# mLSTM cross-attention and fp4 FFN on one core: tiles of 64 tokens of two batches in place of 128 tokens of one

## The chip, the core and the metric

The kernel runs on one core of a Trainium2 chip. Its engines have an instruction stream each: PE (TensorE, matmul), DVE (VectorE), ACT (ScalarE), POOL (GpSimd) and SP (SyncE, which here issues nearly all the DMAs). They wait for one another through semaphores. The metric is the device time of one launch in microseconds (us). All arithmetic outside the quantised matmuls' f16 operands is float32.

## What is computed

`x` and `ctx_1024` are [8, 1024, 512]: 8 batches of 1024 tokens. The attention part is an mLSTM with 8 heads of 64 (NH, DH): queries from layer-normed `x`, keys and values both from `ctx`. The result is added to `x`, layer-normed and sent through a gated FFN 512 -> 1408 -> 512, whose inputs and weights are rounded blockwise to fp4 values.

```python
def attention(q, k, v):                       # q = layernorm(x), k = v = ctx
    gate_in = concat([q, k, v], -1)
    ig = gate_in @ igate_w.T + igate_b;  fg = gate_in @ fgate_w.T + fgate_b   # per head
    log_f_cum = cumsum(log_sigmoid(fg))
    log_D = where(ltr, log_f_cum[s] - log_f_cum[t] + ig[t], -inf)
    m = max(log_D, -1);  D = exp(log_D - m)
    C = (q @ k.T / 8) * D
    n = maximum(abs(sum(C, -1)), exp(-m))
    h = (C / (n + eps)) @ v                   # then a norm over each head, times norm_w
...
y = x + attention(...)
z = fp4_linear(layernorm(y), w_gate), fp4_linear(layernorm(y), w_up)
out = y + fp4_linear(silu(z[0]) * z[1], w_down)
# fp4_linear rounds both operands in blocks of 16: scale = max|x| / 6, grid 0 .. 6
```

The kernel computes attention chunk by chunk: inside a tile with the decay matrix D, and against everything earlier through a state matrix per head (St, 64 x 65: the 65th column is the normalizer) that is decayed and added to after each tile.

## The kernel before

**Tiles.** A tile is 128 tokens (P) of one batch. Tile t belongs to batch t % 8 (its `slot`) and to the chunk t // 8 of 128 tokens, so 64 tiles (NT) and each batch comes back every 8 tiles; `t.has(8)` marks the waits on the state of 8 tiles ago. Heads are handled in pairs: head 2c + par lies in rows 64 par to 64 par + 63 of the array, c from 0 to 3 (HC).

**Turns.** The program is a software pipeline written out by hand. A turn u runs, on each engine, pieces of several tiles: `t0` is tile u, `t1` tile u - 1, and so on to `t11`. A list of calls per engine (`pe_turn`, `dve_turn`, `act_turn`, `pool_turn`, `sp_turn`) is the order; another list per engine (`pe_start` and so on) holds the beginning, in which the weights are quantised as well. No scheduler moves anything: what stands in a list behind a waiting call waits with it.

**PE's turn**: `gu` of t8 (gate and up products, three column pieces, L523), in the middle of it, in every fourth turn, `gate_mm` and `pick_mm` of t1 (L594: gate rows of four tiles are gathered by matmuls with 0/1 matrices); then `u` of t6: L616 is query times old state, in quarters of the array (64 rows x 64 columns), L622 is D times v, 128 rows by 64 columns; then `st_mm` of t6 (L634, the tile's k v products that go into the state), `down` of t9 in three pieces (L654 to L656) with the transpose `row_T` of the gate rows (L501, every fourth turn) after the first, and last `qk` of t5 (L539, the scores). The scores lie in the PSUM banks R0 and R1 (512 columns each, par 0 and 1), u in R2 and R0, the state sums in R1, `down` in a bank of its own.

**DVE** multiplies scores by D (`dve_C`, L1328, one for each par), multiplies gate and up products (`dve_h`, L1336), updates the state (`dve_St`, L1498: new state = old state times a decay + sum, one instruction for each c), and does the larger part of the quantising (`h_lo`, `x_lo` L1387). **ACT** makes D from the broadcast maxima `mb` (`act_D`, L741), applies silu (L794), copies u out of PSUM (`uc`, L935), makes `hz` (L915) and loads function tables: `preload_act_table_set` (L1005) in each turn. **POOL** masks D (`pool_mask`, L1095), scales v (`vc`, `vk`) and the queries (`xw`).

**SP** loads and stores: `xqT` and `hqT` are DMA transposes of the quantised operands, which PE needs for gu and down; `cn` the context rows; `wb` and `mb` the decay rows and maxima, each a row in DRAM broadcast over partitions; `cf`, `xh`, `xb`, `xzb` feed the transposed q and k; `out_dram<-ob` is the store. All loads of x and ctx come straight from the inputs, one per tile of 128 rows.

## Time and profile before

| | |
|---|---|
| three runs | 1754.49, 1754.5, 1754.88 us; median 1754.5 |
| the profiled execution | 1753.9 us, its span 1752.2 us |
| PE busy | 1679.3 us, 96% |
| DVE busy | 1637.0 us, 93% |
| ACT busy | 1297.4 us, 74% |
| POOL busy | 1154.9 us, 66% |
| DMA | 240.60 MB, mean 137 GB/s |

Busy time is the time in which an engine has at least one instruction under way; the rest is waiting. Shares of the whole span are an average over stages, so the rows further down are of single turns and single steps. A line number L with an operation stands for a source line of the kernel, and `out<-in` names the tensors. "xN" counts the records: a float32 matmul leaves two records, an f16 matmul one. The distance from the start of one group of matmuls to the start of the next is what it keeps PE occupied; the duration beside it includes the time in which the last one drains under the next.

### The profile page before, as it was taken

What the parts mean: (1) busy time and instruction counts of PE and PEld (TensorE: products, weight loads), DVE (VectorE), ACT (ScalarE), POOL (GpSimd) and SP (SyncE); (2) the same over time, 40 slices, a digit from 0 to 9 for tenths busy, and PEclk for the clock granted to TensorE, in tenths of its full rate; (3) what the DMA queues carried; (4) which work ended last, traced back from release to release, by engine and by line L of the source; (5) the groups of instructions that cost most, each with busy time, mean ns of one, the idle gap of its engine ahead of it and who ended that gap; (6) DMA issues with size and microseconds to landing.
All of it is one profiled execution on the core that took longest, in us unless ns stands there. A gap on an engine that the chain in (4) does not pass through costs nothing.

```text
span 1752.2 us, 41405 instructions
## 1 busy us (share of the span) xinstructions
PE 1679.3 (96%) x13633; PEld 898.6 (51%) x13633; DVE 1637.0 (93%) x3455; ACT 1297.4 (74%) x2696; POOL 1154.9 (66%) x1188
## 2 busy tenths in 40 slices
PE   4568999999999999999999999999999999999998
PEld 3434555555555555555555555555555555555544
DVE  8998999999999989999998999999899999999996
ACT  7777777777777777787777778777777877767652
POOL 8876767567666766766666666666666666757663
PEclk9689999999999999999999999999999999999999
DMA  6446656566566656656665675665567566654423
GB/s 213 138 95 140 143 140 150 132 149 151 130 153 139 148 133 147 157 132 147 142 143 134 146 160 130 148 144 142 132 149 157 131 147 144 138 113 101 111 68 71
DMA packets 574454, 240.60 MB, mean 137 GB/s; under 512 B 507520, under 2 KB 514176, under 8 KB 574240
## 3 DMA queue, kind: packets, MB, share of 16 engines
q1 hardware_dynamic: 574240, 237.96, 58.4%
q8 instruction: 108, 1.77, 0.4%
q14 instruction: 106, 0.87, 0.2%
HBM read 140.35 MB, written 31.72 MB: 98 GB/s over the span
## 4 chain that ended last, share of the span: by engine, by line
PE 88%; DMA 0%; DVE 0%; ACT 0%; issue 0%; DVEq 0%
PE bank L523 50%; PE bank L654 9%; PE bank L656 8%; PE bank L655 8%; PE bank L622 4%; PE bank L539 4%; PE bank L616 2%; PE bank L634 2%; PE bank L584 1%; PE bank L594 0%; DMA xqT<-xqs 0%; DMA work<-stage 0%; PE bank L501 0%; DVE stage L1312 0%; DVE stage L1336 0%; DVE ob L1294 0%
## 5 line engine op out<-in xcount | busy, mean ns | idle before, releaser
L523 PE MATMUL bank<-wgTh,xqT 128*128 128x512 f16 (+1 forms) x1536 | 556.3, 362 | 7.5 <-DMA xqT<-xqs 6.4
L523 PE MATMUL bank<-wuTh,xqT 128*128 128x512 f16 (+1 forms) x1536 | 555.3, 362 | 0.0
L1102 POOL TENSOR_TENSOR stage<-stage,hs 128x512 f32<-128x512 f32 (+1 forms) x192 | 214.8, 1119 | 140.2 <-DVE stage L1317 138.5
L523 PE MATMUL bank<-wgTl,xqT 128*128 128x512 f16 (+1 forms) x768 | 277.8, 362 | 0.0
L523 PE MATMUL bank<-wuTl,xqT 128*128 128x512 f16 (+1 forms) x768 | 277.8, 362 | 0.0
L654 PE MATMUL bank<-wdTh,work 128*128 128x512 f16 x704 | 267.7, 380 | 3.3 <-DMA work<-stage 3.3
L655 PE MATMUL bank<-wdTl,work 128*128 128x512 f16 x704 | 267.1, 379 | 0.0
L656 PE MATMUL bank<-wdTh,work 128*128 128x512 f16 x704 | 267.0, 379 | 0.0
L523 PEld LDWEIGHTS bank<-wgTh,xqT 128*128 128x128 f16 x1536 | 150.2, 98 | 169.0 <-issue 10.9
L523 PEld LDWEIGHTS bank<-wuTh,xqT 128*128 128x128 f16 x1536 | 150.5, 98 | 147.4 <-issue 0.5
L1157 POOL TENSOR_TENSOR stage<-stage,hinv 128x512 f32<-128x512 f32 (+1 forms) x192 | 212.6, 1119 | 14.1 <-DVE hinv L1416 7.4
L1091 POOL TENSOR_TENSOR sch<-ve,mhalf 128x8 f32<-128x8 f32 x64 | 105.9, 1655 | 165.0 <-DVE ve L1538 164.8
L794 ACT ACTIVATE stage<-bank,wfix 128x512 f32<-128x512 f32 (+1 forms) x192 | 124.7, 649 | 102.6 <-PE bank L523 101.8
L1371 DVE TENSOR_TENSOR stage<-stage 128x512 f16<-128x512 f32 (+1 forms) x192 | 159.1, 829 | 25.2 <-ACT stage L784 25.2
L1140 POOL TENSOR_TENSOR xn<-xn,xs 128x512 f32<-128x512 f32 x64 | 68.8, 1075 | 138.6 <-DVE xn L1383 136.8
L794 ACT ACT_TABLE_LOAD x123 | 157.8, 1283 | 2.4 <-issue 0.3
L741 ACT ACTIVATE D<-mb,cols 128x128 f32<-128x128 f32 x512 | 156.5, 388 | 1.0 <-DMA mb<-max_dram 0.3
L915 ACT ACTIVATE work<-stage 128x512 bf16<-128x512 f32 (+1 forms) x192 | 112.3, 585 | 50.4 <-POOL stage L1157 48.2
L1336 DVE SCALAR_TENSOR_TENSOR stage<-bank,wfix,stage 128x512 f32<-128x512 f32 (+1 forms) x192 | 134.7, 701 | 12.3 <-ACT stage L794 12.3
L1312 DVE SCALAR_TENSOR_TENSOR stage<-work,stage 128x512 f32<-128x512 bf16 (+1 forms) x192 | 123.3, 666 | 7.5 <-ACT work L915 7.3
L800 ACT ACTIVATE xz<-xn 128x512 bf16<-128x512 f32 x64 | 40.2, 628 | 115.2 <-DVE xn L1375 115.2
L1341 DVE TENSOR_REDUCE ham<-stage 128x32 f32<-128x512 f32 (+1 forms) x192 | 121.0, 631 | 1.7
(210 smaller groups left out, 3656.5 us busy)
## 6 DMA issues: line engine op xcount, KB each, us to landing
mb<-max_dram SPq DMA_DIRECT2D x64, 512.0 KB
x<-in_x_dram SPq DMA_DIRECT2D x64, 256.0 KB, 2.9
wb<-warp_dram SPq DMA_DIRECT2D x128, 128.0 KB, 3.1
cn<-in_ctx_dram SPq DMA_DIRECT2D x64, 256.0 KB, 3.1
out_dram<-ob SPq DMA_DIRECT2D x64, 256.0 KB, 2.4
xb<-in_x_dram SPq DMA_DIRECT2D x60, 256.0 KB, 2.8
xh_dram<-xb SPq DMA_DIRECT2D x55, 256.0 KB, 2.3
xzb<-xh_dram SPq DMA_DIRECT2D x220, 64.0 KB, 2.5
```

The lines of the kernel that those rows point to most:

```text
L523: i = e.matmul(o[:, 0:width], x, w[:, c, n0:n0 + width], start=first and k < 2, stop=last and k >= 4)
L654: e.matmul(acc[:, :], hi, wdT[0][:, c0 + c, :], start=(c0 + c == 0), stop=False)
L655: e.matmul(acc[:, :], hi, wdT[1][:, c0 + c, :], start=False, stop=False)
L656: i = e.matmul(acc[:, :], lo, wdT[0][:, c0 + c, :], start=False, stop=(c0 + c == IC - 1))
L741: i = e.activation(D[:, par, c, :], mb[:, h, :], ACT.Exp, bias=bias[:, h:h + 1], scale=-1.0)
L794: e.activation(sl[:, n0:n0 + w], pair(t, n)[0][:, 0:w], ACT.Silu, scale=wfix[:, 0:1]).then_inc(s_silu[n], 1)
L1102: e.tensor_tensor(blocks(hx[:, n0:n0 + w]), blocks(hx[:, n0:n0 + w]), per_block(hs2[:, n0 // BLOCK:(n0 + w) // BLOCK]), ALU.mult).then_inc ...
L1157: e.tensor_tensor(blocks(hx[:, n0:n0 + w]), blocks(hb[:, n0:n0 + w]), per_block(hinv[:, n0 // BLOCK:(n0 + w) // BLOCK]), ALU.mult).then_in ...
L1312: e.scalar_tensor_tensor(hx[:, n0:n0 + w], hz[:, n0:n0 + w], MAGIC, hx[:, n0:n0 + w], ALU.max, ALU.add).then_inc(s_h_t[n], 1)
L1336: e.scalar_tensor_tensor(hb[:, n0:n0 + w], pair(t, n)[1][:, 0:w], wfix[:, 1:2], sl[:, n0:n0 + w], ALU.mult, ALU.mult).then_inc(s_h[n], 1)
L1341: e.tensor_reduce(ham[:, n0 // BLOCK:(n0 + w) // BLOCK], blocks(hb[:, n0:n0 + w]), AX.X, ALU.max, apply_absolute_value=True).then_inc(S_[" ...
L1371: e.tensor_tensor(hqs[n][:, 1, :], hx[:, n0:n0 + w], hqs[n][:, 0, :], ALU.subtract).then_inc(s_h_lo[n], 1)
```

## The change

**Tiles.** A tile holds 64 tokens (S2) of each of two batches, 2p and 2p + 1 with p = t % 4, from chunk t // 4. A pair of batches comes back every 4 tiles, so the state recurrence, and that of the running maximum `mc`, goes over 4 tiles instead of 8. There are 4 state tensors of two batches each in place of 8.

**PE.** Scores of a tile are 64 x 64 for each head and batch: 16 matmuls of a quarter of the array each in place of 8 of half. The new part of u and the state sums are in quarters too, with the contraction over 64 rows instead of 128; the sums of the second batch go into a second bank (`state_sum`), which is a gate bank of tile t - 2, hence the new wait on s_silu1 in st_mm, and one on St in gu. In u the old part of batch 1 runs ahead of that of batch 0, and a wait on PE's own s_u_old stands before the first new one of batch 1. pick_mm is 8 matmuls instead of 2, row_T is 8 instead of one transpose.

**The others.** D is half as large (`mb_D` holds the maxima and D). The two masks cover the lower 64 partitions or all 128, the first has to be done before the second, and both products with D wait for both. The state update is 8 instructions instead of 4, all on DVE. Gate rows are [64, 64] instead of [32, 128]. The table preload runs only in the turns in which the gates of a quad are computed. wb comes in four loads, mb and cn in two, the store in two.

**Staging.** In every fourth turn ACT issues, first of all, five DMAs that copy x and ctx from DRAM to DRAM, `x_tiles` and `c_tiles`, in the tile's order (4 tiles each; tiles from 12 on for x, from 8 on for ctx); the loads of xb, x1, cn and cf then read these copies. The start lists of all engines are reordered in a few places.

```diff
-    max_dram = nc.dram_tensor("max_dram", [NT, NH * P], F32, kind="Internal").ap()
+    max_dram = nc.dram_tensor("max_dram", [NT // 4, GR * S2], F32, kind="Internal").ap()
+    x_tiles = nc.dram_tensor("x_tiles", [NT, P, E], F32, kind="Internal").ap()
+    c_tiles = nc.dram_tensor("c_tiles", [NT, 3 * S2, E], F32, kind="Internal").ap()
...
-        ST = R1[:, 0:HC * DA].rearrange("p (c d) -> p c d", d=DA)
+        def state_sum(t, b):
+            if b == 0:
+                bk = R1[:, 0:HC * DA]
...
+                bk = pair(t.back(2), 1)[0][:, 0:HC * DA]
...
-                e.transpose(RT, rows[:, :], ident[:, :]).then_inc(S_["row_T"], 1)
+                for k in range(2):
+                    e.matmul(RT[HALF[k], 0:GR].rearrange("s (n r) -> s n r", n=2), rows[:, 0, :],
+                             ident[:, :].rearrange("p (n k r) -> p k n r", n=2, k=2)[:, k], start=True, stop=True)
+                for k in range(2):
+                    e.matmul(RT[HALF[k], 3 * QR:4 * QR], rows[:, 1, :], ident[:, GR + QR * k:GR + QR * (k + 1)], start=True, stop=True)
...
+                if t.has(3) and t.back(-1).live(NT):
+                    e.wait_ge(S_["St"], t.done(-1))
...
             for c in range(HC):
-                for par in range(2):
-                    r = slice(par * DH, (par + 1) * DH)
-                    i = e.matmul((R0, R1)[par][:, c * P:(c + 1) * P], cT[r, t.slot, c, :], xT[r, t.slot, c, :], start=True, stop=True)
+                for b in range(2):
+                    for par in range(2):
+                        r = slice(par * DH, (par + 1) * DH)
+                        i = e.matmul((R0, R1)[par][HALF[par ^ b], c * S2:(c + 1) * S2], cT[r, t.slot, c, HALF[b]], xT[r, t.slot, c, HALF[b]],
+                                     start=True, stop=True)
...
-                for k in range(2):
-                    i = e.matmul(gates(t)[1], pick[:, k, :], gpart[:, k, :], start=(k == 0), stop=(k == 1))
+                for out_rows, at in ((gates(t)[1], slice(0, 2 * GR)), (gates(t)[2], slice(2 * GR, 3 * GR))):
+                    for k in range(2):
+                        for b in range(2):
+                            i = e.matmul(out_rows, pick[:, k, b, at], gpart[:, k, HALF[b]], start=(k + b == 0), stop=(k + b == 2))
...
+            def old(c, b):
+                for par in range(2):
+                    r = HALF[par]
+                    i = e.matmul(U[par][HALF[b], c, :], xw[r, b, c, :], St[t.p][r, b, c, :], start=(c == 0), stop=False)
+                return i
+
+            def new(c, b):
+                for k in range(2):
+                    r, par = HALF[k], k ^ b
+                    i = e.matmul(U[par][HALF[b], c, :], D[r, par, c, :], vc[t.parity][r, 2 * c + par, :], start=False, stop=(c == HC - 1))
+                return i
...
-                    i = e.matmul(R1[par * DH:(par + 1) * DH, c * DA:(c + 1) * DA],
-                                 cn[:, h * DH:(h + 1) * DH], vk[:, h, :], start=True, stop=True)
+                    for b in range(2):
+                        h, r = 2 * c + par, HALF[par ^ b]
+                        i = e.matmul(state_sum(t, b)[HALF[par], c, :], cn[r, h * DH:(h + 1) * DH], vk[r, h, :], start=True, stop=True)
...
+        def act_stage_c(e, g):
+            if g > 2:
+                e.wait_ge(S_["c_tiles"], 48 * (g - 2))
+            at = slice(g * S2, (g + 1) * S2)
+            src = ctx_in[:, at, :].rearrange("(p b) s e -> b p s e", b=2)
+            for k in range(3):
+                e.dma_start(c_tiles[4 * g:4 * g + 4, k * S2:(k + 1) * S2, :], src[k % 2]).then_inc(S_["c_tiles"], 16)
+
+        def act_stage_x(e, g):
...
+                e.dma_start(x_tiles[4 * g:4 * g + 4, k * S2:(k + 1) * S2, :], src[k]).then_inc(S_["x_tiles"], 16)
+
         def act_turn(e, u):
             tn = Tile(u + 1)
+            g = (u + 3) // 4
+            if u % 4 == 1 and 4 * g < NT:
+                act_stage_x(e, g)
+                act_stage_c(e, g)
...
-            e.preload_act_table_set(EXP_LN)
+            if t1.live(NT) and t1.slot % 4 == 3:
+                e.preload_act_table_set(EXP_LN)
...
-            e.tensor_tensor(D[:, par, :, :].rearrange("p c s -> p (c s)"), (R0, R1)[par][:, :],
+            e.tensor_tensor(D[:, par, :, :].rearrange("p c s -> p (c s)"), (R0, R1)[par][:, 0:HC * S2],
...
-            for c in range(HC):
-                i = e.scalar_tensor_tensor(St[t.slot][:, c, :], St[t.slot][:, c, :], wb[:, c, P - 1:P], ST[:, c, :], ALU.mult, ALU.add)
+            for b in range(2):
+                for c in range(HC):
+                    i = e.scalar_tensor_tensor(St[t.p][:, b, c, :], St[t.p][:, b, c, :], wb[:, b, c, S2 - 1:S2], state_sum(t, b)[:, c, :], ALU.mult, ALU.add)
```

On PE, u and the state sums of one tile stand so in before's order (the names in brackets are semaphores that the instruction waits for; xN counts the matmuls that follow alike):

```order
L616 MATMUL bank<-St,xw 64x65 [waits s_C0,s_xw,s_St]
L616 MATMUL bank<-St,xw 64x65 x15
L622 MATMUL bank<-vc,D 64x65 [waits s_C1,s_vc]
L622 MATMUL bank<-vc,D 64x65 x15
L634 MATMUL bank<-vk,cn 64x65 [waits s_vk,s_cn_in]
L634 MATMUL bank<-vk,cn 64x65 x7
L654 MATMUL bank<-wdTh,work 128x512 [waits s_out,s_hqT0]
```

and so in the order of the change:

```order
L689 MATMUL bank<-St,xw 64x65 [waits s_C0,s_xw,s_St]
L689 MATMUL bank<-St,xw 64x65 x13
L689 MATMUL bank<-St,xw 64x65 [waits s_C1,s_vc]
L689 MATMUL bank<-St,xw 64x65
L695 MATMUL bank<-vc,mb_D 64x65 x4
L695 MATMUL bank<-vc,mb_D 64x65 [waits s_u_old]
L695 MATMUL bank<-vc,mb_D 64x65 x11
L729 MATMUL bank<-vk,cn 64x65 [waits s_silu1,s_vk,s_cn_in]
L729 MATMUL bank<-vk,cn 64x65 x15
L748 MATMUL bank<-wdTh,work 128x512 [waits s_out,s_hqT0]
```

The wait for the second product with D moved two matmuls ahead, a wait on PE's own work came in between, and the state sums, 16 matmuls for 8, wait for a silu as well.

ACT at the start of a turn with the staging copies, before:

```order
L741 ACTIVATE D<-mb,cols 128x128 x8
L866 ACTIVATE xb<-xb,nb,rs 128x512
L915 ACTIVATE work<-stage 128x512
L927 ACTIVATE mw<-mw,mc 32x128
L756 ACTIVATE nm<-sum 128x1
```

and in the change:

```order
L833 ACTIVATE mb_D<-mb_D,cols 128x64 x8
L1081 DMA x_tiles<-in_x_dram 4x2x16384 x2
L1074 DMA c_tiles<-in_ctx_dram 4x2x16384 x3
L958 ACTIVATE xb<-xb,nb,rs 128x512
L1007 ACTIVATE work<-stage 128x512
L1018 ACTIVATE mw<-mw,mc 64x64
L848 ACTIVATE nm<-sum 128x1
```

Five DMA issues stand ahead of xh (L958) and hz (L1007); the shape of one copy, 4x2x16384, is eight contiguous pieces of 16384 float32.

SP's queue, one turn of before:

```order
L384 DMA_TRANSPOSE xqT<-xqs 128x8x128
L410 DMA cn<-in_ctx_dram 128x512
L402 DMA wb<-warp_dram 64x512 x2
L364 DMA cf<-in_ctx_dram 32x16x32 x4
L345 DMA xh_dram<-xb 128x512
L339 DMA xb<-in_x_dram 128x512
L353 DMA xzb<-xh_dram 32x16x32 x4
L310 DMA out_dram<-ob 128x512
L319 DMA x<-in_x_dram 128x512
L328 DMA_TRANSPOSE work<-stage 128x8x128 x2
L372 DMA mb<-max_dram 128x1024
L328 DMA_TRANSPOSE work<-stage 128x6x128
```

and of the change:

```order
L430 DMA_TRANSPOSE xqT<-xqs 128x8x128
L459 DMA cn<-c_tiles 128x4x64 x2
L449 DMA wb<-warp_dram 64x256 x4
L408 DMA cf<-c_tiles 32x16x32 x4
L387 DMA xh_dram<-xb 128x512
L378 DMA xb<-x_tiles 128x512
L395 DMA xzb<-xh_dram 32x16x32 x4
L341 DMA out_dram<-ob 64x512 x2
L352 DMA x<-x_tiles 128x512
L364 DMA_TRANSPOSE work<-stage 128x8x128 x2
L418 DMA mb_D<-max_dram 64x512 x2
L364 DMA_TRANSPOSE work<-stage 128x6x128
```

The sequence is the same; there are five issues more, and four kinds of load read the staged copies.

## Rows read from the trace of the kernel before

**Rows 1.** The page's first part: busy us, share of the span, instructions.

```profile
PE 1679.3 (96%) x13633; PEld 898.6 (51%) x13633; DVE 1637.0 (93%) x3455; ACT 1297.4 (74%) x2696; POOL 1154.9 (66%) x1188
```

**Rows 2.** The chain that ended last, share of the span by engine.

```profile
PE 88%; DMA 0%; DVE 0%; ACT 0%; issue 0%; DVEq 0%
```

**Rows 3.** Windows of four PE turns: us, busy of PE, PEld, DVE, ACT, POOL, clock, DMA share, GB/s.

```profile
858.54:883.40 24.86, 24.86 (x204) 13.13 (x203) 24.55 (x52) 19.85 (x43) 17.59 (x19) 1.00 0.70 158
883.40:908.26 24.86, 24.86 (x204) 13.13 (x203) 23.97 (x51) 18.81 (x40) 16.83 (x18) 1.00 0.65 149
908.26:933.12 24.86, 24.86 (x204) 13.12 (x203) 23.86 (x51) 18.82 (x40) 16.71 (x18) 1.00 0.64 146
933.12:960.50 27.38, 27.38 (x241) 14.61 (x240) 23.86 (x57) 20.29 (x46) 15.75 (x17) 1.00 0.53 122
```

**Rows 4.** Timeline of PE: start us, duration us, line, operation, stationary and moving shapes, records.

```profile
806.25 1.16 PE L539 MATMUL bank<-xT,cT 64*128 64x128 f32 x16
807.34 0.39 PE L523 MATMUL bank<-wgTh,xqT 128*128 128x512 f16 x1
...
821.71 0.70 PE L616 MATMUL bank<-St,xw 64*64 64x65 f32 x32
822.33 1.15 PE L622 MATMUL bank<-vc,D 128*64 128x65 f32 x32
823.32 0.64 PE L634 MATMUL bank<-vk,cn 128*64 128x65 f32 x16
823.89 0.39 PE L654 MATMUL bank<-wdTh,work 128*128 128x512 f16 x1
...
845.52 0.60 PE L594 MATMUL bank<-gpart,pick 128*96 128x128 f32 x4
845.96 0.33 PE L523 MATMUL bank<-wgTh,xqT 128*128 128x384 f16 x1
...
853.76 0.27 PE L501 MATMUL bank<-ident,rows 128*128 128x128 f32 x1
853.87 0.38 PE L654 MATMUL bank<-wdTh,work 128*128 128x512 f16 x1
```

**Rows 5.** Groups by form, DVE: total busy us, mean ns of one, idle before.

```profile
L1336 DVE SCALAR_TENSOR_TENSOR stage<-bank,wfix,stage 128x512 f32<-128x512 f32 x128 | 95.3, 744 | 12.0 <-ACT stage L794 12.0
L1336 DVE SCALAR_TENSOR_TENSOR stage<-bank,wfix,stage 128x384 f32<-128x384 f32 x64 | 39.4, 616 | 0.3 <-ACT stage L794 0.3
L1328 DVE TENSOR_TENSOR D<-bank,D 128x512 f32<-128x512 f32 x128 | 86.5, 675 | 1.8 <-POOL D L1095 1.8
L1498 DVE SCALAR_TENSOR_TENSOR St<-St,wb,bank 128x65 f32<-128x65 f32 x256 | 55.0, 277 | 0.9 <-issue 0.6 <-PE bank L634 0.3
```

**Rows 6.** The same view, ACT's table preload.

```profile
L1005 ACT ACT_TABLE_LOAD x61 | 78.3, 1283 | 1.1
```

**Rows 7.** Timeline around xqT and nr; the third is the page's DMA landing.

```profile
801.54 0.68 DVE L1387 TENSOR_TENSOR xqs<-xn,xqs 128x512 f16<-128x512 f32 x1
...
802.25 1.24 SPq L384 DMA_TRANSPOSE xqT<-xqs  x1
...
xqT<-xqs SPq DMA_TRANSPOSE x64, 3.1
...
824.22 0.17 DVE L1508 SCALAR_TENSOR_TENSOR nr<-uc,cols 128x8 f32<-128x8 f32 x1 [0.60 <-ACT uc L935]
```

**Rows 8.** Timeline: SP's issue of cn, silu 1, and hz with DVE's next step.

```profile
803.58 0.53 SPq L410 DMA_DIRECT2D cn<-in_ctx_dram  x1
...
849.53 0.69 ACT L794 ACTIVATE stage<-bank,wfix 128x512 f32<-128x512 f32 x1
...
859.25 0.63 ACT L915 ACTIVATE work<-stage 128x512 bf16<-128x512 f32 x1 [0.20 <-POOL stage L1157]
...
861.25 1.28 DVE L1312 SCALAR_TENSOR_TENSOR stage<-work,stage 128x512 f32<-128x512 bf16 x2
```

**Rows 9.** The page's DMA part: queue and kind, packets, MB, share of 16 engines.

```profile
q8 instruction: 108, 1.77, 0.4%
```

300 lines of the change are left out of this document (182 added, 118 removed).

## The prediction

> **What bounds the kernel now.** I read four views, in this order. The shares of busy time name two candidates: PE is busy for 96% of the span and DVE for 93% [rows 1]. The chain of work that ended last settles it: 88% of it is PE, the rest spread thin [rows 2]. The windows of four successive turns show how: PE is busy in every nanosecond at full clock, turns of 24.86, 24.86, 24.86 and 27.38 us, 101.96 us together, while DVE has 24.55, 23.97, 23.86 and 23.86 us of work in them [rows 3]. So DVE idles 0.3 to 1.0 us in three turns and 3.5 in the fourth, the one with the gates. What a step costs PE I take from the timeline as the distance from its start to the start of what follows, since matmuls overlap [rows 4]. The 64 tiles make 16 such cycles, of which I count 14 with all their steps; start and end cut the other two. One microsecond off PE in each turn is therefore worth 64 us, as long as everything that PE waits for also comes earlier. The other engines' distances to PE are the question, so I read them last [rows 6, 7, 8].
>
> **PE, each turn.** The scores take 806.25 to 807.34 = 1.09 us for 16 records of 64 rows by 128 columns [rows 4]. After: 32 records in array quarters. The old-state part of u is such a case, 32 records on quarters in 821.71 to 822.33 = 0.62 us [rows 4]. I take 0.62: **-0.47 us**. The two others that change form are the new part of u, 0.99, and the state sums, 0.57 [rows 4]. With the old part they cost 2.18. After, all three are 32 records of the quarter form, 3 x 0.62 = 1.86 if the halves overlap as in the old part. The staggered order leaves half of the array idle at both ends of u, and its new wait on PE's own work (s_u_old) drains part of the pipe; 2 of 16 steps at 0.04 each is 0.08. So 1.94: **-0.24 us**, between -0.1 (a full drain of 0.14 more) and -0.35. Together -0.71 a turn (-0.6 to -0.85).
>
> **PE, each fourth turn.** pick goes from two matmuls, 4 records in 0.44 us [rows 4], to eight, 16 records, with 64 moving columns instead of 128. At the old 0.11 each they cost 1.76 (+1.3), at half of it 0.88 (+0.4). I take +0.8, since the moving side has half the columns but the stationary side stays as tall. row_T goes from one transpose in 0.11 us (853.76 to 853.87 [rows 4]) to eight matmuls, 16 records, none over 64 columns wide; at the quarter form's 0.02 to 0.04 each that is 0.3 to 0.7, so +0.45 (0 to 0.6). Together +1.25 (+0.4 to +1.9, mostly 0.9 to 1.7).
>
> PE's sum for four turns is -2.84 + 1.25 = -1.6 us: 14 x -1.6 = **-22 us** (-13 to -30).
>
> **DVE.** A width of 512 in place of 384 costs 744 - 616 = 128 ns in one of its operations [rows 5], 0.13 us per 128 elements. The two products with D go from 512 to 256: -0.27 each, -0.54. The state update doubles from four instructions to eight; each is 277 ns busy [rows 5], but four take 0.86 us, so one more costs about 0.2 from start to start: +0.86. Each turn gets **+0.3 us**; the gate operations, 64 columns for 128, give some 0.35 back in the fourth, an estimate: five of them at half of the 0.13. DVE then needs 24.85, 24.3, 24.2 and 23.8 us, where PE's turns are 24.15 (24.86 - 0.71) three times and 27.9 once. DVE falls behind by 0.7 + 0.1 = 0.8 us and catches up in the gate turn. Whether PE feels that depends on the margins. The transpose of xqT is issued when x_lo ends at 802.22 and takes 3.1 us to land, 805.4, against its use at 807.34 [rows 4, 7]: 2.0 us. qk, 0.47 shorter, now lies in this stretch, which leaves 1.5. The 0.8 fits in. What follows u on DVE (nr) does not come late by itself: it waits 0.60 us for ACT, which waits for PE [rows 7], and moves with PE.
>
> **ACT.** The decay's exponentials have half the columns, which I cost at nothing, since nothing waits for them. The table preload of 1.28 us, once a turn now [rows 6], and the reload that it forces stay only in each fourth turn: 2.57 us less in three turns. ACT has 19.9 of 24.86 us of work [rows 3], so nothing of it is on the path, but ACT's answers to PE come a little sooner. At the start of each fourth turn it issues the five staging copies. SP's issue of a 256 KB load took 0.53 us [rows 8], five make 2.6 us, and they stand ahead of xh, of hz 1 and hz 0, for which DVE's next step waits [rows 8]. The work queued there now runs at 859.25; I take it that about 1.0 us of delay reaches DVE (0 if ACT is early, 2.6 if all of it counts), on top of the 0.8 above: 1.8 against a margin of 1.5. Other margins are as thin in that turn (silu 1 ends at 850.22 and st_mm, which waits for it after, starts at 850.59 [rows 4, 8], 0.37 us). I put the give-back at 0.7 us a cycle, 12 cycles with copies: **+8 us** (0 to +15).
>
> **SP's queue.** Its loads of rows split in two where they were one, five issues more a turn (wb two, mb, cn and stored one each), at some 0.55 [rows 8]. cn, wb, cf, xh and xb stand behind one another, so xb's load comes 3 x 0.6 = 1.8 us later; SP idles longer than that ahead of it, and hqT 0 and 1 wait for DVE's h_lo, behind all of these. I cost it at nothing; if SP is late at hqT 0, PE's down waits by up to 1 us a turn, which is part of the second rival. mb moves half the bytes: -256 KB a turn.
>
> **Start and end.** The start lists get three more groups of copies, and fewer and shorter steps: -1 us (-5 to +5).
>
> **Sum.** The profiled run took 1753.9 us (span 1752.2 and 1.7 around it), 0.6 below the median of 1754.5; it fits. 1753.9 - 22.3 + 8 - 1 = **1738.6, say 1739**, own range 1724 to 1750.
>
> **Rival A, the staging copies hold up the transposes: 1830 us.** Each group is 40 pieces of 64 KB from DRAM to DRAM, 2.5 MB. The only packets of comparable size in the trace are those of the instruction queue: 108 of 1.77 MB, 16.4 KB each, and 0.4% of 16 x 1752 us is 112 us, so 1.04 us each [rows 9]. A piece of 64 KB would take 4.2 us. For it: forty of them fill 16 DMA engines for 10.4 us, and fewer engines for longer; the transposes of xqT and hqT, which land in 3.1 us [rows 7], are needed within 5; whatever queues behind even one piece is 4 us late. Against it: DMA is at 0.70 to 0.53 of its capacity [rows 3], which leaves 38 us of all engines idle in a cycle for 10.4, and the loads wait for nothing if the engines serve them between the pieces. If loads wait for the whole group, 10.4 us less the margins of 2 to 3 is 5 to 10 us of idle PE: 12 x 5 = +60 to 12 x 10 = +120, here 1739 + 90 = 1829, say 1830 (1799 to 1859, more if few engines carry the copies). It decides once a transposing load's landing goes from 3.1 to above 5 us.
>
> The Trainium skill ("DMA: Bandwidth & Descriptors", section "Why a DMA increments its semaphore by 16 and not by 1") says that a transfer uses as many engines as the largest number up to 16 that divides its slowest dimension. The copies' slowest dimension is 4; by that rule four engines would carry ten pieces each, an estimate of 42 us, and this rival would reach 1900. The same page's section "Queues, rings and completion order" says that an engine takes turns between queues packet by packet, which would soften it; no row of before shows a copy of this shape.
>
> **Rival B, DVE and the queues take all back: 1752 us (1748 to 1762).** DVE is then 0.3 us a turn dearer and has no room left: 97.1 us of work in a PE cycle of 100.3. If its work has gaps that it can't close in the gate turn, because C, h and St wait there for PE in any case, each cycle gives back 1.2 us instead of 0.7, and SP's lateness at hqT adds 0.1 to 0.2 in each turn, 0.6 a cycle: 14 x 0.5 + 14 x 0.6 = 15 less what is counted twice, 1739 + 13 = 1752. For it: DVE idles only 0.3 us in the first turn [rows 3]. Against it: 3.5 us idle in the gate turn.
>
> **Rival C, quarters don't overlap where both row halves write one bank: 1785 us.** In the new part of u and in the state sums of after, both row halves of the array fill the same bank, in different partitions. In before each row half has a bank of its own in the quarter form, so no row shows the case. If only two of four quarters then run at a time, 32 records cost what 32 with two in flight cost now: 0.99 for the new part, 2 x 0.57 = 1.14 for the sums [rows 4]. Against 0.62 each that is 0.37 + 0.52 = +0.89 a turn, 64 x 0.89 = 57; PE's turns are then no shorter than today, DVE keeps up, and the 8 us of give-back fall away: 1739 + 57 - 8 = 1788, some 1785 with the stagger's 0.08 not counted twice.
>
> The Trainium skill ("TensorEngine Tiling (Array Packing)", section "Restrictions and Gotchas", Gotcha 1) says that different row tiles can't use one PSUM bank at the same time. By that rule rival C would be the outcome; no row of before tells.
>
> **How the numbers follow.** "Same" is within 0.2%, 3.5 us around 1754.5, about what a measurement of this kernel can tell from no change. The forecast has 0.53: 0.50 faster and 0.03 in its tail above 1751. A has 0.25, all slower; the windows of [rows 3] leave room for the copies, but nothing in before shows their form. B has 0.12: 0.02 faster, 0.05 same, 0.05 slower. C has 0.05, slower. A time below 1724 (pick and row_T at their low ends, no give-back) has 0.03, and something slower that I don't see 0.02. Faster 0.50 + 0.02 + 0.03 = 0.55; same 0.03 + 0.05 = 0.08; slower 0.25 + 0.05 + 0.05 + 0.02 = 0.37. The range runs from 1724, the forecast's low end, to 1850: it takes in B, C and most of A, and leaves out 0.03 below and some 0.1 of A above.
>
> **What would show it.** Right: windows of four PE turns with PE still busy throughout, 24.15 three times and near 28; qk's line 0.62 from start to start; u and the state sums 1.94; three of four preloads gone; DVE's idle in the first three turns near zero. A: PE idle behind xqT or hqT in the turn of the copies, their landings above 5 us, DMA share near 1 for 10 us or long packets on a few engines, turns of over 30 us there and forecast turns elsewhere. B: gaps of PE before gu 0, u or down, released by DVE, in turns without copies too. C: u and the sums at 2.5 us or more together. I am wrong outright if PE's turns are no shorter though PE is gapless, or if PE's clock falls in gaps of the copy turn, as it does nowhere in before [rows 3].

## The result, and the profile after

The changed kernel takes **2185.6 us** (median; 2180.0 to 2189.5) beside 1754.5 for the kernel before on the same chip: a ratio of **1.246 (1.243 to 1.249)**, 431 us slower. The forecast was 1739, the range 1724 to 1850. The profiled run took 2180.0, its span 2178.2.

The page of the changed kernel: first part (busy us, share of the span, instructions), the chain that ended last by engine, and queues (packets, MB, share of 16 engines' span).

```profile
PE 1733.5 (80%) x16113; PEld 906.8 (42%) x16113; DVE 1781.6 (82%) x3711; ACT 1153.3 (53%) x2602; POOL 1158.4 (53%) x1196
issue 58%; POOL 32%; DVE 3%; SPq 2%; PE 2%; DMA 2%; ACT 1%; POOLq 1%; DVEq 0%; ACTq 0%
...
q10 hardware_dynamic: 816, 35.65, 3.9%
```

PE held 88% of the chain before [rows 2] and has 2% now. "Issue" is time in which the engine waited for nothing that the profile shows; it holds 58%, so much of the chain has no releaser that the profile names, and the windows have to tell more. Here are two turns of the changed kernel (columns as in [rows 3]), one without and one with the staging copies:

```profile
1404.77:1431.55 26.78, 25.59 (x240) 12.94 (x239) 26.47 (x55) 16.13 (x37) 16.77 (x17) 1.00 0.65 127
...
1462.47:1507.35 44.88, 37.06 (x336) 19.37 (x334) 30.95 (x67) 21.09 (x49) 17.93 (x18) 0.96 0.44 119
```

Against the 24.86 us of [rows 3] there are two different losses. The turn with the copies takes 44.9 us, with PE and DVE both idle for long and the DMA share low. But a turn *without* copies also takes 26.8, and there DVE is busy for 26.47 of 26.78 us: DVE has become the bound, by 2.6 us a turn more than its 23.9.

I cut every span at two starts of scores, that of the ninth tile and that of the last. In the tables "start" is what lies ahead of the first, "mid" between the two, "end" the rest (profiled run, us; start and end to within 0.7). The ratio is against the kernel before on the same chip; its interval is worth 2 to 7 us on either side.

| kernel | median | ratio (95%) | start | mid | end |
|---|---|---|---|---|---|
| before | 1754.5 | | 271.6 | 1400.2 | 80.4 |
| after | 2185.6 | 1.246 (1.243 to 1.249) | 363.0 | 1729.3 | 85.9 |

### The profile page after: what moved, and what is told of

Same layout as the page of the kernel before. It is cut to its first block, busy times and chain, and to the rows that moved or that the text cites. A ratio compares the mean times of both kernels' runs of the same rounds, so it can differ in the third digit from the quotient of the medians.

```text
span 2178.2 us, 47128 instructions
## 1 busy us (share of the span) xinstructions
PE 1733.5 (80%) x16113; PEld 906.8 (42%) x16113; DVE 1781.6 (82%) x3711; ACT 1153.3 (53%) x2602; POOL 1158.4 (53%) x1196
## 3 DMA queue, kind: packets, MB, share of 16 engines
q10 hardware_dynamic: 816, 35.65, 3.9%
## 4 chain that ended last, share of the span: by engine, by line
issue 58%; POOL 32%; DVE 3%; SPq 2%; PE 2%; DMA 2%; ACT 1%; POOLq 1%; DVEq 0%; ACTq 0%
POOL stage L1273 6%; POOL stage L1218 4%; POOL mb_D L1211 4%; POOL xw L1251 3%; POOL un L1284 3%; POOL xn L1256 3%; POOL vk L1243 3%; POOL vc L1235 2%; POOL rs L1262 1%; SPq L478 1%; PE bank L592 1%; SPq L465 1%; DMA cf<-in_ctx_dram 1%; POOL nb L1266 0%; DMA xqT<-xqs 0%
## 5 line engine op out<-in xcount | busy, mean ns | idle before, releaser
L592 PE MATMUL bank<-wgTh,xqT 128*128 128x512 f16 (+1 forms) x1536 | 572.3, 373 | 131.4 <-DMA xqT<-xqs 74.7
L592 PE MATMUL bank<-wuTh,xqT 128*128 128x512 f16 (+1 forms) x1536 | 570.2, 371 | 0.0
L592 PE MATMUL bank<-wgTl,xqT 128*128 128x512 f16 (+1 forms) x768 | 285.5, 372 | 0.0
L592 PE MATMUL bank<-wuTl,xqT 128*128 128x512 f16 (+1 forms) x768 | 285.3, 371 | 0.0
L1436 DVE SCALAR_TENSOR_TENSOR stage<-work,stage 128x512 f32<-128x512 bf16 (+1 forms) x192 | 252.9, 1344 | 2.3
L689 PE MATMUL bank<-St,xw 64*64 64x65 f32 x2048 | 54.5, 248 | 186.8 <-DVE mb_D L1447 174.0
L934 ACT ACTIVATE junk<-xb 128x512 bf16<-128x512 f32 x60 | 37.8, 629 | 304.5 <-DMA xb<-x_tiles 293.7
L1235 POOL TENSOR_TENSOR vc<-cn,cols 128x512 f32<-128x512 f32 x64 | 66.8, 1043 | 223.4 <-DMA cn<-c_tiles 194.9
L1741 DVE STREAM_TRANSPOSE cT<-cf 128x512 f32<-128x512 f32 x55 | 38.4, 698 | 175.3 <-DMA cf<-c_tiles 175.3
L1431 DVE SCALAR_TENSOR_TENSOR stage<-work,stage 128x512 f32<-128x512 bf16 (+1 forms) x192 | 118.6, 644 | 40.2 <-ACT work L1007 40.0
L1007 ACT ACTIVATE work<-stage 128x512 bf16<-128x512 f32 (+1 forms) x192 | 112.1, 584 | 69.1 <-POOL stage L1273 68.8
L1490 DVE TENSOR_TENSOR stage<-stage 128x512 f16<-128x512 f32 (+1 forms) x192 | 120.4, 627 | 31.1 <-ACT stage L876 31.1
```

The lines of the kernel that those rows point to most:

```text
L592: i = e.matmul(o[:, 0:width], x, w[:, c, n0:n0 + width], start=first and k < 2, stop=last and k >= 4)
L1007: e.activation(hz[:, n0:n0 + w], hx[:, n0:n0 + w], ACT.Abs, scale=FP4_ONE).then_inc(s_hz[n], 1)
L1431: e.scalar_tensor_tensor(hx[:, n0:n0 + w], hz[:, n0:n0 + w], MAGIC, hx[:, n0:n0 + w], ALU.max, ALU.add).then_inc(s_h_t[n], 1)
L1436: e.scalar_tensor_tensor(hx[:, n0:n0 + w], hz[:, n0:n0 + w], MAGIC, hx[:, n0:n0 + w], ALU.max, ALU.subtract).then_inc(s_h_q[n], 1)
L1490: e.tensor_tensor(hqs[n][:, 1, :], hx[:, n0:n0 + w], hqs[n][:, 0, :], ALU.subtract).then_inc(s_h_lo[n], 1)
```

## The experiments

### The staging copies

**The changed kernel without its copies (e1).** The loads of rows read x and ctx directly. In e1 and in every run built on it (e5, e7, e9, e10, e12) they fetch rows of other tokens, so these runs price the steps but don't compute the result.

```diff
-    act_stage_x(e, g); act_stage_c(e, g)      # here and in the start list
-    e.dma_start(xb[:, :], x_tiles[t.first])
+    e.dma_start(xb[:, :], x_flat[at_flat(t, 0, P), :])   # x1, c alike
```

> The change without the staging copies: xb, x1, cn and cf are loaded with the same shapes and the same number of DMAs straight from x and ctx, from the places of before's tiles (so the data belong to other tokens, and the output is not the reference's), and ACT issues no DMA. Theory A, the copies are the whole loss: PE-bound turns come back and the time is my forecast without the give-back, 1725 to 1745. Theory A + P, the copies are one part and the other is that DVE is held up by POOL in three of four turns (the second h_q takes 3.97 us instead of 0.69 there): the cycle of four turns is then 3 x 26.8 + 30.9 = 111.3 us against 101.96 before, and the time 1754 + 14 x 9.3 = 1885 (1860 to 1900). Rival, the copies cost nothing and loads wait for something else: 2180.

1937.6 us, 1.105 (1.103 to 1.107); start 312.1, mid 1533.9, end 84.8. So the copies are worth 248 us (195 mid, 51 start), and **183 us are left that have nothing to do with them**. That lies outside all three ranges expected; the nearest, which has both copies and a stall of DVE, had 131 us left.

**The kernel before with the same copies (e4),** into DRAM that nobody reads.

```diff
 def act_turn(e, u):
+    g = (u + 3) // 4
+    if u % 4 == 1 and 4 * g < NT:
+        act_copies(e, g)      # the five DMAs of one group
```

> The kernel before with the change's copies added and nothing else: twelve groups of five DMAs, 4x2x16384, issued by ACT at the start of each fourth turn, into DRAM that nobody reads. If the copies alone stop the loads on the engines that they share, each group costs what the change's copy turn is longer than its neighbours, 44.9 - 26.8 = 18 us, and up to 20 since before has no idle time: 1754 + 12 x 18 to 20 = 1970 to 1995. If the loss comes only from loads that wait for the copied tiles, or from SP's extra loads, it is 1755 to 1770.

2077.8, 1.185 (1.182 to 1.187); start 299.5, mid 1699.5, end 79.9. That is above the 1970 to 1995 expected. Only the turn with the copies changes, from 24.86 to some 52 us: 12 x 27 = 324. Two rows of this kernel's trace, the first gate-up matmul of a turn with copies and the waits view (total us, times, longest), and the source view's landing times of the transposing load:

```profile
1044.69 0.61 PE L526 MATMUL bank<-wgTh,xqT 128*128 128x512 f16 x1 [24.67 <-DMA xqT<-xqs]
PE bank L526 <- DMA xqT<-xqs: 304.3, 16, 34.4
DMA to landing us min/median/max: 3.0/3.1/38.5
```

The median of [rows 7] still stands, but the longest is 38.5 us: the condition of rival A. In the changed kernel the same load's longest is 13.8, and more of the loss lies in what SP issues. Its queue in the turn with the copies (start us, duration us, line, operation):

```profile
1481.61 1.23 SPq L430 DMA_TRANSPOSE xqT<-xqs  x1
1482.94 1.50 SPq L459 DMA_DIRECT2D cn<-c_tiles  x2
1484.55 22.85 SPq L449 DMA_DIRECT2D wb<-warp_dram  x4
```

And ACT's queue beside the first of these, one of its five copies:

```profile
1482.11 0.62 ACTq L1081 DMA_DIRECT2D x_tiles<-in_x_dram  x1
```

ACT gets rid of its DMAs in 0.6 us each, as forecast. SP, half a microsecond later, needs 22.85 us to issue four loads that take about half a microsecond apiece elsewhere [rows 8]. What SP has behind them, cf and xb, is issued some 20 us late. cn, issued before them, lands late: its longest landing is 28.7 us, its median 2.8 (source view of L459). The waits of the changed kernel name their users:

```profile
ACT junk L934 <- DMA xb<-x_tiles: 293.7, 51, 23.9
POOL vc L1235 <- DMA cn<-c_tiles: 194.9, 11, 19.1
DVE cT L1741 <- DMA cf<-c_tiles: 175.3, 12, 18.2
PE bank L689 <- DVE mb_D L1447: 174.0, 13, 20.3
```

cn and cf: 11 and 12 waits of up to 19 and 18 us, about one for each group. PE stands behind DVE, DVE behind cf.

**The copies on 16 engines (e2), and in smaller pieces on four (e3).**

```diff
 # e2: q=16 (16 x 4 x 2048 elements); e3: q=4 (4 x 4 x 8192)
-e.dma_start(x_tiles[...], src[k])
+e.dma_start(x_tiles[...].rearrange("p (q s) e -> q p (s e)", q=16),
+            src[k].rearrange("p (q s) e -> q p (s e)", q=16))
```

> The change with the same bytes copied in the same five DMAs from the same place, only that each is laid out as 16x4x2048 instead of 4x2x16384: sixteen groups of four pieces of 8 KB in place of eight pieces of 64 KB. If what stands still is the four DMA engines that carry the large pieces (40 pieces of 2.42 us on four engines, 25 us), the copies spread over sixteen and take about 6 us, SP's queue doesn't stand, and the time is that of the run without copies within 1.5%: 1885 to 1910. If the copied bytes themselves or ACT's five issues are the cost, it stays above 2050.

> The change with each copy laid out as 4x4x8192: the same bytes, pieces of 32 KB instead of 64 KB, and the slowest dimension still 4. If the number of engines is what matters, forty becomes eighty pieces of half the time on the same four engines, the 25 us stay and so does the time: 2160 to 2190. If the size of a piece is what blocks a load behind it, the loads wait half as long each and the time falls half of the way to the 16x4x2048 form: 2060 to 2100.

e2: 1964.9, 1.120 (1.116 to 1.123); start 321.0, mid 1555.9, end 86.2; the median is above the 1885 to 1910 expected. e3, as expected if the engines count: 2179.8, 1.241 (1.237 to 1.246), that is unchanged; 366.5, 1729.2, 85.7. The copies' queue in e2, then in e3:

```profile
q10 hardware_dynamic: 5440, 35.66, 5.3%
```

```profile
q10 hardware_dynamic: 1360, 35.65, 3.9%
```

The changed kernel moves 35.65 MB in 816 packets. 35.65 MB are 544 pieces of 64 KB; the other 272 are 68 copies x 4. In e2 there are 5440 = 68 x (64 + 16), in e3 1360 = 68 x (16 + 4). The part that doesn't grow with the pieces reads as one packet for each engine that a copy uses: 4, 16, 4. The time agrees: 3.9% of 16 x 2178.2 us is 1359 us over 544 pieces, **2.5 us a piece**; a group is 40 pieces, on four engines 25 us; in e2 5.3% of 16 x 1963.1 us, over 13.6 groups and 16 engines, is 7.7 us. So e3 is as slow as the kernel it was made from, though its pieces are smaller, and e2 gets 221 of 248 us back. The number of engines decides; halving the pieces on the same four does nothing. e2's pieces are also smaller, 8 KB, and that size on four engines was not run. The Trainium skill ("DMA: Bandwidth & Descriptors", section "Why a DMA increments its semaphore by 16 and not by 1") gives the rule, the largest number up to 16 that divides the slowest dimension of both sides; here, with a slowest dimension of 4, 16 and 4, the trace agrees in all three.

The records of single packets show how the loads are held up. In the changed kernel a window out of a group of copies (columns as in [rows 3]) has a DMA share of 0.25, four engines of 16:

```profile
1488.00:1504.00 16.00, 13.42 (x57) 5.99 (x58) 7.39 (x15) 4.32 (x8) 3.56 (x4) 0.89 0.25 103
```

All through it three or four pieces of 64 KB are under way, 2.42 us each, and ahead of each of the 28 that start from 1489.7 to 1504.9 us one packet of 256 B of SP's queue is served. So the four engines do take turns between the two queues, but one small packet waits for one large piece. From 1495.0 to 1504.3 SP's queue moves 18 packets of 256 B and nothing else. The new loads of cn consist of such packets, 512 each (128 x 4 runs of 64 float32). Over 16 engines that is 32 per engine, an estimate, where ten pieces on each of the four and five semaphore writes leave room for some 15. In e3 there are 20 pieces and as many writes on each, still fewer than 32, and the longest landing of cn is 28.1 us; in e2 it is 11.9. The Trainium skill (same page, section "Queues, rings and completion order") lets an engine take turns between its queues packet by packet, and this trace agrees. Why SP's *issuing* stands as well, up to 12 us for one load, is open.

### What is left without copies: 183 us

In e1 DVE is again the engine that is full (94% of the span). One place stands out in every kernel with the changed code. In the changed kernel, DVE's stretch around the scores at 884.45, and POOL's beside it:

```profile
884.15 1.28 DVE L1431 SCALAR_TENSOR_TENSOR stage<-work,stage 128x512 f32<-128x512 bf16 x2
885.47 4.58 DVE L1436 SCALAR_TENSOR_TENSOR stage<-work,stage 128x512 f32<-128x512 bf16 x2
```

```profile
885.33 0.55 POOL L1226 TENSOR_TENSOR rs<-ss,mhalf 128x1 f32<-128x1 f32 x1 [1.73 <-ACT ss L869]
885.84 0.83 POOL L1211 TENSOR_SCALAR_AFFINE_SELECT mb_D<-mb_D 64x512 f32<-64x512 f32 x1
886.65 1.05 POOL L1218 TENSOR_TENSOR stage<-stage,hs 128x512 f32<-128x512 f32 x1
887.66 0.83 POOL L1273 TENSOR_TENSOR stage<-stage,hinv 128x384 f32<-128x384 f32 x1
888.46 1.04 POOL L1235 TENSOR_TENSOR vc<-cn,cols 128x512 f32<-128x512 f32 x1
```

The two halves of h_q at L1436 take 4.58 us together, 1.3 for the pair at L1431. The second of them alone lasts 3.97 us, not 0.69: it ends at 890.05, 0.55 us after POOL's run of back-to-back instructions (888.46 + 1.04). DVE instructions of over 2 us after the first 250 us: none in the kernel before, 47 in the changed one, 58 in e1, 249 us together in e1. Each of these 105 ends 0.04 to 0.55 us after the end of a run of POOL.

Four things could do this: the order of the work on POOL, the eight state updates, the missing table preloads (ACT answers earlier), and the masks, of which the second now covers 64 partitions. One run each.

**POOL's order (e5).** e1 with the h_qs that waits for DVE put first.

```diff
 # pool_turn: as before for the masks and rs2, then
+    pool_h_qs(e, t9, 1)
     pool_h_qs(e, t9, 0)
     pool_hx(e, t9, 2)
     pool_vc(e, t6)
-    pool_h_qs(e, t9, 1)
     pool_xw(e, t6)
```

> The run without copies (data of other tokens, as there) with one edit in POOL's turn: h_qs 1 is called ahead of h_qs 0, so that POOL waits for DVE's second h_q instead of running mask, h_qs 0, hx 2 and vc without a gap while DVE stands. If POOL's unbroken run is what holds DVE up for 3.3 us, the second h_q takes under 1.5 us, DVE has room again and the time falls by up to 14 x 3 x 2.7 = 113 to 139 us, at most down to PE's own pace: 1735 to 1780. If DVE is simply out of room because of the eight state updates, the order changes nothing or costs: 1870 to 1900.

1853.6, 1.057 (1.055 to 1.059); 309.5, 1458.1, 84.7. 84 us less, between the two ranges expected. Long instructions fall from 58 to 18: the 40 or so on h_q are gone, and what is left is on xs (4.99 us each), which was long 17 times in e1 as well. Where POOL's run starts and what DVE has there matters; why it shuts DVE out is not told by this.

**The state updates: e1 with four of eight (e7), the kernel before with four more (e6).**

```diff
 # e7, dve_St
-for b in range(2):
+for b in range(1):
 # e6, dve_St of the kernel before
+for c in range(HC):
+    e.scalar_tensor_tensor(Sx[:, c, :], St[t.slot][:, c, :], wb[:, c, P - 1:P], ST[:, c, :], ALU.mult, ALU.add)
```

> The run without copies (data of other tokens), with the state update of the second batch left out, so that DVE issues four updates as before instead of eight and the second batch's state stays zero. If the doubled update is what makes DVE late and sets off the stall, the second h_q falls back to 0.7 us and the time to PE's pace and the longer start: 1754 - 22 + 40 = 1772, 1760 to 1800. If the stall comes from ACT and POOL being earlier in their turn (half the decay matrix, no preload), it stays and only 0.8 us a turn is saved: 1938 - 50 = 1885.

> The kernel before with four more state-update instructions on DVE in each turn, into a tile that nobody reads: DVE's added load of the change, alone. By the sum of my prediction DVE then needs 25.4, 24.8, 24.7 and 24.7 us in turns of 24.86 three times and 27.4 once, it gives back in the gate turn, and the time is 1754 to 1765. If DVE, once late against POOL by half a microsecond, is shut out for the length of POOL's unbroken run, turns go to 26 to 27 us in three of four: 1754 + 14 x 5 to 8 = 1825 to 1866, and the line of the second h_q shows durations near 3 to 4 us.

e7: 1911.4, 1.090 (1.087 to 1.092); 311.9, 1515.2, 82.9; 57 long instructions, nearly all on xs now. e6: 1773.7, 1.012 (1.010 to 1.014); 274.1, 1416.9, 81.9; none. Four updates cost 19 to 26 us, 0.3 to 0.4 a turn, and cause no stall. e7 saves half of what was expected even without the stall going, e6 costs more than the 0 to 11 expected.

**The table preloads: e1 with one each turn (e9), the kernel before with one each fourth (e8).**

```diff
 # e8; e9 is the reverse
+if t1.live(NT) and t1.slot % 4 == 3:
     e.preload_act_table_set(EXP_LN)
```

> The run without copies (data of other tokens) with the preload back in each turn. If the missing preload is what lets POOL overtake DVE, the second h_q falls back to 0.7 us and the time to 1790 to 1850, with the longer start. If the order of events is set elsewhere (half the decay matrix, the masks, DVE's longer update), it stays at 1930 to 1945.

> The kernel before with the table preload only in the turns with gates, as in the change, and nothing else. If ACT, 2.6 us less busy in three turns, brings POOL's run of six instructions ahead of DVE's second h_q, before gets the same stall and the time rises by 1 to 2 us in each of these turns: 1790 to 1850. If the preload has no part in it (its 1.28 us lie in ACT's idle time): 1750 to 1756.

e9: 1923.2, 1.097 (1.095 to 1.098); 310.7, 1525.9, 84.6; 57 long ones. e8: 1754.0, 1.000 (0.999 to 1.001); 271.1, 1400.2, 81.7. Not this either: 14 us in the one, where at least 88 were expected of a cause, nothing in the other. Leaving out three of four table loads brings the kernel before nothing.

**The mask over 128 partitions (e10), and the kernel before with a mask over 64 (e11).** A small edit each; both leave values of D masked wrongly.

```diff
 # e10, on e1
-part = mb_D[0:S2 * (k + 1), 1, :, :]
+part = mb_D[:, 1, :, :]
 # e11, on the kernel before
+n = P if par else P // 2
-e.affine_select(out=D[:, par, :, :], in_=D[:, par, :, :], ...
+e.affine_select(out=D[0:n, par, :, :], in_=D[0:n, par, :, :], ...
```

> The run without copies (data of other tokens) with the second mask of each tile over 128 partitions instead of 64 (so that rows 64 to 127 of the decay matrix are masked wrongly); the order of all calls is unchanged. All 58 stalls of DVE above 2 us in the run without copies began in a POOL run with this mask in it, and kernels with masks over 128 partitions alone had none. If an instruction over 64 partitions is what keeps DVE out of the gaps in POOL's run, the stalls above 2 us vanish and the time falls by 2 to 3 us a turn: 1938 - 56 x 2.5 = 1800 (1790 to 1850). If it is the timing alone, the stalls stay and so does the time, 1925 to 1945.

> The kernel before with its second mask (par 0) over 64 partitions instead of 128, so that the rest of that half is left unmasked; nothing else. If the 64-partition form is what keeps DVE out, xs, which waits 0.7 us in before, waits for the whole of POOL's run, 4 to 5 us, in every turn: DVE then needs 28 us a turn, 1754 + 56 x 3 = 1920 (1850 to 1960). If the form has no part in it: 1750 to 1757.

e10: **1794.6**, 1.024 (1.022 to 1.026); 307.7, 1403.0, 82.0; no long instruction. e11: **1908.0**, 1.088 (1.086 to 1.090); 287.1, 1537.4, 81.8; 57 of them. Both are as expected if the form is the cause. Widening this one mask to 128 partitions takes 143 us off e1, narrowing it to 64 adds 154 us to the kernel before, and the long instructions go and come with it. In e10 the same place reads, on DVE and on POOL:

```profile
1052.55 1.75 DVE L1436 SCALAR_TENSOR_TENSOR stage<-work,stage 128x512 f32<-128x512 bf16 x2
```

```profile
1052.91 0.84 POOL L1211 TENSOR_SCALAR_AFFINE_SELECT mb_D<-mb_D 128x512 f32<-128x512 f32 x1
1053.73 1.48 POOL L1218 TENSOR_TENSOR stage<-stage,hs 128x512 f32<-128x512 f32 x1
```

The instructions meet in the same way; but now DVE gets in after the mask, the pair takes 1.75 us, and POOL's next instruction lasts 1.48 instead of 1.05. The mask itself is no slower over 128 partitions than over 64 (0.84, 0.83). In e11 the victim is xs, which the source view gives as min/median/max ns; the kernel before, then e11, and POOL's run in e11 beside one such xs:

```profile
L1357 DVE TENSOR_SCALAR xs<-xam,rs x64: 227/924/928, 102.0 to 1701.6; 128x32 f32<-128x32 f32 x64
```

```profile
L1358 DVE TENSOR_SCALAR xs<-xam,rs x64: 229/4973/5486, 105.5 to 1856.2; 128x32 f32<-128x32 f32 x64
```

```profile
994.75 4.97 DVE L1358 TENSOR_SCALAR xs<-xam,rs 128x32 f32<-128x32 f32 x1
...
993.89 0.72 POOL L1096 TENSOR_SCALAR_AFFINE_SELECT D<-D 64x512 f32<-64x512 f32 x1
```

The Trainium skill ("SBUF — State Buffer", section "SBUF: two separate sides") says that GpSimd and DVE (in an operation with two SBUF inputs, or in a two-port mode) hold a shared port for a whole instruction, and that the other fully blocks. e10's rows agree: the pair ends at 1054.30, 0.55 us after the mask. The 3.97 and 4.97 us do not: there DVE waits for the end of a run of several instructions. In both runs the mask is the second, right behind a short rs of 128x1. Why an instruction over 64 partitions there does that is open.

### What is left without copies and stall

**e1 with both causes out of the way (e12):** the masks back to back ahead of rs2, where DVE doesn't meet them, e5's order, and in PE's start list the state sums of the third tile ahead of its gate-up.

```diff
 # pool_turn
     pool_mask(e, t6, 1)
+    pool_mask(e, t6, 0)
     pool_rs2(e, t7)
-    pool_mask(e, t6, 0)
 # PE's start list
-pe_gu(e, T[1], 0); pe_st_mm(e, T[2])
+pe_st_mm(e, T[2]); pe_gu(e, T[1], 0)
```

> The run without copies (data of other tokens) with three edits: the two masks one behind the other, h_qs 1 ahead of h_qs 0, and the state sums of tile 2 ahead of gu 0 of tile 1 in the start. It shows what PE's saving is worth when neither copies nor long stalls are there. If the saving of my sum is real, three turns are 24.05 to 24.5 us and the cycle is 100.5 to 101.5 against 101.97, with 38 us of start on top: 1775 to 1795. If DVE is what sets the pace even so, the cycle is above 102.5 and the time 1800 to 1815.

1790.7, 1.021 (1.019 to 1.023); 308.0, 1398.8, 83.2; no long instruction. **The mid part is as long as before (1400.2), and nearly all that is left, 36 us, lies in the start.** Four turns in e12:

```profile
1021.20:1045.40 24.20, 24.17 (x245) 12.47 (x235) 23.89 (x54) 15.88 (x36) 16.03 (x18) 1.00 0.73 135
1045.40:1070.50 25.10, 24.38 (x242) 12.51 (x233) 24.79 (x55) 16.30 (x37) 16.92 (x18) 1.00 0.62 136
1070.50:1099.10 28.60, 28.34 (x309) 15.43 (x298) 27.20 (x64) 20.76 (x47) 18.27 (x19) 1.00 0.59 127
1099.10:1123.10 24.00, 24.00 (x243) 12.40 (x233) 23.73 (x53) 16.18 (x39) 15.67 (x17) 1.00 0.67 136
```

101.90 us, where [rows 3] have 101.96. PE is busy for 100.89; the best turns are as forecast, 24.0 to 24.2, but DVE has 99.6 us of work, not the forecast's 97.1. The groups of DVE in this window of e12 (busy us, mean ns), and behind them those of the kernel before in the same window:

```profile
L1613 DVE SCALAR_TENSOR_TENSOR St<-St,wb,bank 128x65 f32<-128x65 f32 x32 | 6.5, 275 | 0.0
L1496 DVE SCALAR_TENSOR_TENSOR xn<-xz,xn 128x512 f32<-128x512 bf16 x4 | 5.7, 1421 | 0.0
L1526 DVE TENSOR_SCALAR hs<-ham 128x88 f32<-128x88 f32 x5 | 5.3, 1054 | 0.0
L1445 DVE TENSOR_TENSOR mb_D<-bank,mb_D 128x256 f32<-128x256 f32 x8 | 3.3, 411 | 0.0
```

```profile
L1328 DVE TENSOR_TENSOR D<-bank,D 128x512 f32<-128x512 f32 x8 | 5.4, 675 | 0.0
L1379 DVE SCALAR_TENSOR_TENSOR xn<-xz,xn 128x512 f32<-128x512 bf16 x4 | 4.1, 1036 | 0.8 <-ACT xz L800 0.8
...
L1498 DVE SCALAR_TENSOR_TENSOR St<-St,wb,bank 128x65 f32<-128x65 f32 x16 | 3.4, 278 | 0.0
L1409 DVE TENSOR_SCALAR hs<-ham 128x88 f32<-128x88 f32 x4 | 0.8, 193 | 0.0
```

Its own work moved as costed: updates +3.1, the products with D -2.1. But hs takes 1054 ns instead of 193 with the same shape, xn 1421 instead of 1036. These are operations that meet POOL elsewhere in the turn than they used to: 4 x 0.86 + 4 x 0.39 = 5.0 us, of which some is given back in others (xs has its 924 no more). One hs of e12 and POOL beside it:

```profile
1045.61 1.06 DVE L1526 TENSOR_SCALAR hs<-ham 128x88 f32<-128x88 f32 x1
1045.23 2.39 POOL L1273 TENSOR_TENSOR stage<-stage,hinv 128x512 f32<-128x512 f32 x2 [0.42 <-DVE hinv L1533]
```

After the first 300 us, 57 of the 59 hs of e12 start while POOL is in its product with hinv, take 1.0 us or more and end 0.06 to 0.07 us after that instruction (the row above holds two of them). In the kernel before only 7 meet it so, and take 1.0 us too; 48 start during the short nb ahead of it and take 0.2.

**The start: the kernel before with the doubled loads of its first tiles (e13).**

```diff
 # x, x1 (first 12 tiles) and cf in two DMAs, cn (first 8) in four
+for b in range(2):
+    e.dma_start(xb[HALF[b], :], half_rows(x_rows, t, b))
```

> The kernel before with the change's number of loads in the start: x and x1 of tiles below 12 and cf of the first in two DMAs each, cn of tiles below 8 in four; the same bytes, all issued by SP. If SP's queue, which issues without a pause from 110 to 170 us, is what makes the change's start 38 to 40 us longer, this gives 20 to 40 us: 1775 to 1795. If it is the order of the start lists or DVE's waits, 1754 to 1765.

1769.4, 1.010 (1.007 to 1.012); 282.3, 1400.2, 81.8, between the two ranges expected. The start gets 10.7 us longer by the split loads alone (the whole span 12, the median 15): more issues, and cn in runs of 256 B. Mid is untouched. SP is busy issuing for 48 of the 60 us from 110 to 170 in the kernel before. Its transposing load of the second tile's xqT leaves at 133.84 us there, in e13 at 140.97:

```profile
133.84 2.62 SPq L384 DMA_TRANSPOSE xqT<-xqs  x1
```

```profile
140.97 1.24 SPq L398 DMA_TRANSPOSE xqT<-xqs  x1
```

Some 25 us of the start stay unexplained. They are there early: the scores of the fourth tile start at 135.5 us in the kernel before, at 140.7 in e13, at 157.9 in e12.

### Versions that compute everything

**v2:** e2's copies spread over four turns (two of x, then one of ctx in each of three), with e5's order. **v3:** v2 with e12's masks and start. **v4:** v3 with DVE's xs behind xi. **v6:** v3 with one mask for both halves, a product with a stored triangle of zeros and ones over 128 partitions. **v7:** v6 with the state's decay on ACT (eight activations with a scale), and two additions instead of eight updates on DVE.

```diff
 # v6, pool_mask
-e.affine_select(out=part, in_=part, ...)          # twice
+keep = tri[:, :].unsqueeze(1).broadcast_to([P, NH, S2])
+e.tensor_tensor(whole, whole, keep, ALU.mult)     # once
 # v7, act_decay and dve_St
+i = e.activation(St[t.p][:, b, c, :], St[t.p][:, b, c, :], ACT.Identity, scale=wb[:, b, c, S2 - 1:S2])
+i = e.tensor_tensor(St[t.p][:, b, :, :], St[t.p][:, b, :, :], state_sum(t, b), ALU.add)
```

> A complete version: the change with copies of the form 16x4x2048, two in the first turn of four and one in each of the others instead of all five in one, and POOL's turn with h_qs 1 ahead of h_qs 0. If the copies' remaining cost is their density and ACT's five issues in one turn, it comes near the run without copies in the same POOL order, 1854: 1855 to 1880. If each copy costs wherever it stands, it is that plus what separates the 16-engine form from no copies (27 us): 1880 to 1900.

> The complete version with 16-engine copies spread over the turns and POOL's h_qs 1 first (1872 us), with two more edits: POOL runs the two masks one behind the other ahead of rs2, and in PE's start list the state sums of tile 2 stand ahead of gu 0 of tile 1. If the mask between rs2 and h_qs is what still holds DVE's second h_q up for 1.05 us, three turns of four get shorter by up to 1 us, 14 x 3 = -42 at most; DVE waits 9.8 us for those state sums in the start, -5 to -10. So 1820 to 1855. If DVE meets POOL's run elsewhere instead, 1862 to 1875.

> The version before this one with DVE's xs moved behind xi, six instructions later. In the turn behind the gates xs takes 4.99 us instead of 0.55, under POOL's run from mask to xw; of the six instructions that now come first none was held up there for more than 0.6 us. If they run under POOL's run, that turn gains 2 to 3 us: 14 x 2.5 = -35 against the run before. If the hold-up only moves to h_lo, which reads two SBUF operands too, nothing is gained.

> A complete version: 16-engine copies spread over the turns, POOL's h_qs 1 first, the start edit, and in place of the two masks one multiplication of the decay matrix by a stored 0/1 triangle over 128 partitions. POOL saves 0.9 us a turn and runs no instruction over 64 partitions. By the run without copies in the good order (1791) plus what spread copies cost (1872 - 1854 = 18): 1800 to 1815. If DVE's products and POOL's new two-operand instruction hold each other up, 1820 or more.

> The version before this one with the state update shared: ACT multiplies the two states by their decay (eight short instructions behind sq, 1.6 us of its idle time) and DVE adds the sums in two instructions of 260 elements, 0.8 us instead of 1.6. If DVE's load is what keeps the turns above 24.05, the cycle falls from some 102.5 towards PE's 100.4: 14 x 2 = 28 us, 1775 to 1790. If the margins of copies, ACT and POOL set it, nothing or a loss: 1800 to 1820. Neither is expected to beat before, since the start alone costs 37 us.

| kernel | median | ratio (95%) | start | mid | end |
|---|---|---|---|---|---|
| v2 | 1871.7 | 1.068 (1.066 to 1.070) | 313.7 | 1470.7 | 84.9 |
| v3 | 1822.5 | 1.040 (1.038 to 1.042) | 316.0 | 1420.4 | 81.7 |
| v4 | 1823.5 | 1.040 (1.038 to 1.041) | 314.2 | 1422.2 | 83.7 |
| v6 | 1825.8 | 1.042 (1.039 to 1.044) | 315.3 | 1427.2 | 84.0 |
| v7 | 1883.0 | 1.076 (1.072 to 1.080) | 318.0 | 1481.7 | 82.4 |

Spreading seems to bring the copies' price from 27 us (e2 against e1) to 18 (v2 against e5). But in the better order, v3 against e12, the same spread copies cost 32 (8 start, 22 mid), so spreading is not shown to help. v3 is the best complete one, 363 us faster than the change as it was made and still 4% slower than the kernel before: 44 us in the start, 20 mid. v4 gains nothing. v6 has no mask over 64 partitions and is no better than v3, which has no long instruction either. v7 takes work from DVE, but lands far above both of its ranges: DVE now waits for ACT's silu, 79.3 us in all, where in v6 it waits 17.4:

```profile
DVE stage L1481 <- ACT stage L887: 79.3, 68, 2.5
```

## Why the prediction was wrong, step by step

The 431 us come in three parts: copies 248 (changed kernel less e1), the 64-partition mask 143 (e1 less e10), and 40 that e10 has over the kernel before, 36 of them in the start. They add up because each is taken from the kernel that the one before it left; in another order the parts differ (in the kernel before the copies cost 324, the mask 154).

**PE, each turn: right.** The changed kernel's PE, from start to start (columns as in [rows 4]):

```profile
884.45 0.69 PE L609 MATMUL bank<-xT,cT 64*64 64x64 f32 x32
885.08 0.39 PE L592 MATMUL bank<-wgTh,xqT 128*128 128x512 f16 x1
...
899.44 0.74 PE L689 MATMUL bank<-St,xw 64*64 64x65 f32 x32
...
901.27 0.39 PE L748 MATMUL bank<-wdTh,work 128*128 128x512 f16 x1
```

The scores take 0.63 us (forecast 0.62), u and the sums 1.83 (forecast 1.94, within its bounds of 1.83 to 2.08). The best turns are 24.0 to 24.2 (forecast 24.15).

**PE, each fourth turn: right.** In e12:

```profile
1084.23 1.61 PE L670 MATMUL bank<-gpart,pick 128*128 128x64 f32 x16
1085.77 0.34 PE L595 MATMUL bank<-wgTh,xqT 128*128 128x384 f16 x1
...
1093.32 0.34 PE L560 MATMUL bank<-ident,rows 128*64 128x64 f32 x4
1093.90 0.39 PE L751 MATMUL bank<-wdTh,work 128*128 128x512 f16 x1
```

pick 1.54 (+1.10, forecast +0.8, in its bounds), row_T 0.58 (+0.47, forecast +0.45). With 28.25 for such a turn a cycle of PE alone is 100.4, where the working gave 100.36. That it fits so closely is luck: the three turns came out some 0.3 us shorter together, the fourth 0.35 longer.

**DVE: the mechanism was right, the size was not, and the step "the 0.8 fits in" failed.** The +0.3 a turn of its own work held. What I left out is that the durations of [rows 5 to 7] hold beside the POOL work of *their* place. A change that shifts DVE against POOL re-prices operations that it doesn't touch: hs and xn, 5 us a cycle, net 2.5 more than forecast. DVE then needs 99.6 us in a PE cycle of 100.4, with no room for a wait, and the 22 us that PE saves are gone (mid 1398.8 against 1400.2). Rival B named this end for the steady state, DVE without room, but took 13 of the 22 us back and for other reasons; it had 0.12.

**What no step had: 143 us by the mask over 64 partitions.** The change names the mask, and the prediction has no term for POOL at all; its rows say that POOL is idle 7 us a turn. The mask itself takes 0.83 us over 64 partitions as over 128. The step that failed is that the sum gave every DVE instruction a price that doesn't depend on what POOL does beside it.

**ACT's share of the copies: priced at the wrong end.** The issue took 0.6 us each, as costed, and the forecast's +8 us was made of that. The cost lies in the transfer, and in SP, which I had "at nothing": four loads take 21 to 24 us to issue in each of 12 turns.

**Rival A: right in its mechanism, with too low a price.** Rival A named the copies, the loads behind them and the landing of over 5 us (13.8 in the changed kernel, 38.5 in e4). I chose against it on "the loads wait for nothing if the engines serve them between the pieces". The engines do serve them between the pieces, and that is the step that failed: one packet goes between two pieces, so a load of many packets is held for as long as the copies last. The price went wrong in two terms that half cancel: 2.5 us a piece, not 4.2, but on 4 engines, not 16, so 25 us a group, not 10.4. Less the margins of 2 to 3 that is 22; the mid part lost 195 us, 18 for each of the 11 groups in it, where the rival had 5 to 10, and the start, with three groups (one without x), lost 51 more. The sentence with the skill's rule had four engines and 42 us a group, 1900 in all; its engines were right, and with the trace's 2.5 us a piece in place of my 4.2 it comes to the measured 25.

**Rival C: false.** Both row halves write one bank, and the three sets of 32 records, one with separate banks and two without, take 1.83 us together, not the 2.5 or more of the rival. The Trainium skill ("TensorEngine Tiling (Array Packing)", "Restrictions and Gotchas", Gotcha 1), by which different row tiles can't use one PSUM bank at a time, is not borne out by this trace.

**Start and end: wrong.** -1 (-5 to +5) was forecast, +36 came in the start without any copies and +2 to +3 in the end. The step that failed is "fewer and shorter steps": the loads of the first tiles are split, which e13 shows to cost 11 us. The rest is open.

**PE's clock** was said to be a sign of error if it fell, and it did, in the standstill of a turn with copies. The clock falls to 0.50, the lower of its two levels (1.2 GHz). Windows of the changed kernel, the last of PE's work, and then PE at rest:

```profile
856.00:860.00 4.00, 1.04 (x7) 0.39 (x4) 0.00 (x0) 0.00 (x0) 0.00 (x0) 0.88 0.32 82
860.00:864.00 4.00, 0.00 (x0) 0.00 (x0) 0.84 (x2) 0.00 (x0) 3.04 (x3) 0.50 0.53 124
```

## What to carry to other kernels

Where a change adds a transfer of a new shape, first count the engines that it uses, and ask what stands behind it in *every* queue, not only in the one that issues it; sixteen engines instead of four, with smaller pieces, brought 221 of 248 us back. Where DVE is nearly full, a duration from the trace is valid only beside the POOL work that it met there: list, for each POOL instruction that moves or changes its shape, which DVE instruction it will now meet. A saving on the bound engine is worth what the second engine leaves of it, here 1 of 22 us.

## What the runs showed of the hardware that I had not expected

- A POOL instruction over 64 partitions, second in an unbroken run, kept DVE out until the run ended: 3.97 us for a 0.69 us instruction (changed kernel), 4.97 for 0.92 (e11). Over 128 partitions DVE got in at the next instruction (e10: 1.75 us for the pair). One mask, 0.83 us long either way, was worth 143 and 154 us.
- Copies from DRAM to DRAM with a slowest dimension of 4 ran on four engines, 2.5 us for each 64 KB piece. On these engines another queue got one 256 B packet through for each piece (28 of 28 pieces in one stretch), its loads landed up to 28.7 us after issue (median 2.8), and issuing four of them took 22.85 us. Pieces half as long on the same four engines changed nothing (2179.8 against 2185.6, 1.241 against 1.246).
- A DVE instruction of 0.19 us that started inside a POOL instruction ended 0.06 us after it, at 1.05 us (57 times in e12).
- Array quarters of both row halves that write one PSUM bank cost no more than those with a bank each: 0.61 us for each set of 32 records.
